# Four partial loads of the next half image, a new order on VectorE, and high parts written by ScalarE in a normalised DCT and ODE-solver kernel

## The chip, the cores and the metric

The kernel runs on one core of one Trainium2 chip. The metric is the device time of one execution in microseconds (us); the median of three runs before is 3626.96 us.

## The reference, cut to what matters

Sixteen images of 32 channels and 112x112 pixels. First a normalised 2-D cosine transform is added to the input, then six Euler steps of a small network with two 3x3 convolutions and three group normalisations (one channel per group, so instance normalisation).

```python
def _L0_conv_ref(x):
    y = jnp.einsum('kh,bchw->bckw', Dh, x)
    return jnp.einsum('lw,bckw->bckl', Dw, y)

def odefunc(t, y):
    h = jax.nn.relu(_group_norm(y, gn1_w, gn1_b))
    h = _concat_conv(t, h, conv1_w, conv1_b)
    h = jax.nn.relu(_group_norm(h, gn2_w, gn2_b))
    h = _concat_conv(t, h, conv2_w, conv2_b)
    return _group_norm(h, gn3_w, gn3_b)

def step(y, t):                       # six times, dt = 1/6
    return (y + dt * odefunc(t, y), None)

x = x + _L0_conv_ref(_gn(x))
x = x + _L1_conv_ref(_gn(x), ...)     # returns y after six steps
```

## The kernel before

**Tiling.** Two images are in work at a time, one in each of two slots; eight groups of two images make the sixteen. An image of a slot lies on 128 partitions as 32 channels times four pixel parities. A convolution is TensorE matmuls over f16 operands. Each activation is held as a high part (f16 of the f32 value) and a low part (f16 of what is left); products high x high, high x low and low x high are summed in PSUM. A convolution call (`convolve`) goes through eight pieces in the order of `PHASES`: X0 X1 Y0 X2 Y1 X3 Y2 Y3, where the number is one of four parts of the image. An X piece has 12 rounds of four matmuls, a Y piece 6. A dict `between` puts other matmuls at a (piece, round). X of part k waits until the low parts up to k+2 (`lo_done`) are there.

**Staging.** `step(g, s, kind)` exists once for each engine; s is the solver step, 0 to 5. Its four convolution calls are: slot 1 conv 1, slot 0 conv 2, slot 1 conv 2, and slot 0 conv 1 of the next solver step. The two slots alternate, so that the normalisation of one is worked out while TensorE convolves the other. For one convolution call the chain is: ScalarE evacuates PSUM to z (`evacuate`); VectorE takes statistics (`pair_stats`), or for conv 2 ScalarE sums squares (`squares`) and VectorE products with y (`products`); TensorE sums them over partitions (`statistics`); VectorE works out scale and bias, with one or two rsqrt on GpSimd (`post`, `post_state`); ScalarE applies scale, bias and relu (`activate`), VectorE subtracts to get the low part (`split`). With `hi=True`, `activate` also writes the f16 high part before it writes the f32 value in place; with `hi=False`, VectorE's `split` makes the high part with a cast.

**Kinds of step.** In the first seven groups steps 0 to 3 are MID: they also carry the transform of one half of a later image (16 channels). This work is: load of xs, `half_stats` (one batch-norm statistics instruction a channel), `half_pre`, `half_post`, `normalise_first` on VectorE for the first four channels and `normalise` on GpSimd for the other twelve, `dct_rows` and `dct_columns` on TensorE in the fourth call, `batch_copy` on ScalarE, and `half_add` (called `added(b)` in the step), which reads xs and writes x1s. Step 4 is FOUR, step 5 FIVE (both prepare the next group's start states). The last group has LAST_MID steps and a LAST.

**Queues.** All DMAs are issued by SyncE, in program order. In each MID step these are `last_piece` (loads of an earlier result half, a wait for VectorE's `last_add`, the out store), `store_half` (L384), which waits until all four `half_add` of the half are done, and `load_half` (L370), which waits for the same and loads all of xs. VectorE waits for it before `half_stats(range(0, 4))`, behind `pre_of(Z1, 0, 9)` and ahead of `post_of(Z1, 0)`. The order on each engine is written out by hand in `step`; every engine is in order.

**Where the lines lie.** Cast of a high part on VectorE L1085, low part L1089, Euler update L1093, products L1101, statistics of xs L1138, `half_add` L1187; on ScalarE evacuation L667, squares L687, high parts L696, relu in f32 L697; `post_state` begins at L1039. TensorE: convolution matmuls L1456, statistics of Z2 L1550, of Z1 L1544.

Of the kernel before, what the change touches and what calls it, by code (L numbers as in the profile page):

```python
# [28 lines left out]
NP = 4  # L29
# [43 lines left out]
HI_ACT, HI_DVE = 10, 6  # L73
# [68 lines left out]
def build(nc, x, wt, w0, par, dct_c, mats_c, coef_c, ind_c, x1d, yd, out):  # L142
# [5 lines left out]
    with ExitStack() as ctx:  # L148
# [107 lines left out]
        xsb_in = sem("xsb_in")  # L256
        s_m0 = sem("s_m0")
# [99 lines left out]
        def _(sp):  # L357
# [9 lines left out]
            def load_half(index, n):  # L367

                sp.wait_ge(x1_done, NBATCH * n + 1)
                sp.dma_start(xs[:], x_half[bass.ds(index, 1)].rearrange("a h c w -> (a h) c w")).then_inc(xs_in, 16)  # L370
# [59 lines left out]
            load_half(HALVES % NHALF, HALVES)  # L430
# [12 lines left out]
            with sp.Fori(0, LG) as g:  # L443
                with sp.Fori(0, HALVES) as s:
                    with sp.If(g > 0):
                        last_piece(g, g * HALVES + s)
                    store_half((g + 1) * HALVES + s)
                    load_half(((g + 1) * HALVES + s + 1) % NHALF, (g + 1) * HALVES + s + 1)
# [45 lines left out]
            sp.wait_ge(xs_in, 16 * (first_place(HALVES * GROUPS) + 1))  # L494
# [154 lines left out]
        def _(act):  # L649
# [96 lines left out]
            def step(g, s, kind):  # L746
# [43 lines left out]
                activate(1, Z1, 0, False)  # L790
                squares(0, 0, c, sq + 0)
                activate(1, Z1, 1, False)
                evacuate(0, 1, s, 1, 1, c)
                activate(1, Z1, 2, False)
                squares(0, 1, c, sq + 1)
                evacuate(0, 1, s, 1, 2, c)
                activate(1, Z1, 3, False)
# [65 lines left out]
        def _(dve):  # L863
# [169 lines left out]
            def post_state(slot, ev, n, covs, meanwhile):  # L1033
# [16 lines left out]
                                               op0=ALU.mult, op1=ALU.subtract, reverse1=True).then_inc(cov_done, 1)  # L1050

# [83 lines left out]
            def half_stats(channels, buffers=FIRST):  # L1135
                src, _, _, bn0, _ = buffers
                for c in channels:
                    ins = nc.vector.bn_stats(bn0[:, c, :], src[:, c, :])  # L1138
                if channels[-1] == CQ - 1:
                    ins.then_inc(s_m0, 1)  # L1140

# [103 lines left out]
            def step(g, s, kind, adds=False):  # L1245
# [19 lines left out]
                def split_for(phase, k):  # L1265
# [3 lines left out]
                    if phase == 1:  # L1269
                        by_act = HI_ACT * u + k  # L1270
                    elif phase == 2:
                        by_dve = 2 * NP + HI_DVE * u + k
                    elif phase == 3 and k < 2:
                        by_dve = 2 * NP + HI_DVE * u + NP + k
                    elif phase == 3:
                        by_act = HI_ACT * u + NP + k - 2
                    else:
                        by_act = HI_ACT * u + NP + 2 + k
                    split(slot, conv, k, conv_at(g, s, phase), by_act, by_dve)

                def update(slot, meanwhile):

                    if keeps:
                        post_state(slot, stats_before(g, s, kind) + STATS[kind].index((Z2, slot)),
                                   posts_before(g, s, kind) + POSTS[kind].index((Z2, slot)),
                                   2 * (5 * g + s) + slot, meanwhile)
# [9 lines left out]
                if kind == MID:  # L1296
                    dve.wait_ge(xs_in, 16 * first_place(hn) + 16)
                    half_stats(range(0, 4))
# [3 lines left out]
                if kind == MID:  # L1302
                    half_stats(range(4, 7))
                split_for(1, 1)
                stats_of(0, 1)
                if kind == MID:
                    half_stats(range(7, 10))
# [38 lines left out]
                if kind == MID:  # L1346
                    normalise_first(hn)
# [3 lines left out]
                euler(0, 2)  # L1351
                if kind == LAST:
                    euler(0, 3)
# [4 lines left out]
                split_for(3, 0)  # L1358
                split_for(3, 1)
                products_of(2, 0)  # L1360
# [57 lines left out]
        def _(pe):  # L1418
# [179 lines left out]
            def step(g, s, kind):  # L1598
# [38 lines left out]
                between = {(1, 10): lambda: statistics_of(Z2, 0)}  # L1637
# [59 lines left out]
```

## Time and profile before

| | before |
|---|---|
| median of 3 runs | 3626.96 us (3626.53 to 3645.11) |
| profiled execution | 3623.7 us |
| its span | 3621.9 us |
| TensorE matmul / weight load busy | 83% / 70% |
| VectorE, ScalarE, GpSimd busy | 75%, 69%, 28% |
| mean granted clock of TensorE | 0.936 |
| DMA | 217.55 MB, mean 60 GB/s |

A matmul's end is modelled, so a busy share of 83% is an upper figure; the start times of matmuls show where TensorE stood. In a timeline, the bracket behind an instruction gives the idle time of its engine before it and the instruction that ended it. A row of the statistics by windows gives the length of a stretch, then the busy time of each engine with its count of instructions.

### The profile page before, as it was taken

To read this page: it belongs to the slowest core of one execution; us is meant where nothing else is said; L and a number is where in the kernel's file an instruction comes from. 1 tells how busy PE (TensorE), PEld (TensorE's weight loads), DVE (VectorE), ACT (ScalarE), POOL (GpSimd) and SP (SyncE) were. 2 spreads that over 40 slices of the span, in tenths; PEclk is the share of its full clock that TensorE was granted. 3 is DMA by queue.
4 is the path that set the end of the run, shared out by engine and by line. 5 is a ranking of instruction groups with operands and counts; after the bars stand their busy time and mean duration, and the time that the engine had idled before them with its cause. 6 is when DMAs were issued, how large, how long until landed. Compare 5 with 4: busy or idle time off the path is not lost.

```text
span 3621.9 us, 147894 instructions
## 1 busy us (share of the span) xinstructions
PE 3012.7 (83%) x61716; PEld 2531.6 (70%) x61716; DVE 2723.5 (75%) x6289; ACT 2497.7 (69%) x3867; POOL 1012.9 (28%) x1293
## 2 busy tenths in 40 slices
PE   3589888888888888888988888888888888889984
PEld 3477777767777677776777767677777676778873
DVE  6577777777777777776877678777886777768883
ACT  0376678666786667866787567866678666787774
POOL 4034411443124331333313333133421344111111
PEclk7799999999999999999999999999999999999997
DMA  4300033111331131322303213141132211330113
GB/s 85 81 21 21 20 56 92 47 47 56 56 93 47 56 79 24 92 63 75 65 3 101 82 47 65 23 116 47 47 65 57 82 47 47 65 91 30 56 47 108
DMA packets 368816, 217.55 MB, mean 60 GB/s; under 512 B 353152, under 2 KB 353520, under 8 KB 366064
## 3 DMA queue, kind: packets, MB, share of 16 engines
q1 hardware_dynamic: 368112, 207.63, 22.9%
q8 instruction: 507, 8.31, 0.9%
q14 instruction: 197, 1.61, 0.1%
HBM read 104.85 MB, written 77.07 MB: 50 GB/s over the span
## 4 chain that ended last, share of the span: by engine, by line
issue 40%; DVE 17%; ACT 14%; PE 12%; POOL 11%; DMA 3%; SPq 2%; POOLq 1%; DVEq 0%; ACTq 0%
PE cps L1456 8%; ACT z L697 5%; ACT z L667 4%; DVE y L1093 3%; POOL m L547 3%; DVE ha L1089 2%; SPq L439 2%; DVE hb L1089 2%; POOL small L504 2%; POOL ha L535 2%; DMA y<-xa 1%; PE dps L1564 1%; ACT unread_z L687 1%; DVE unread_yz L1101 1%; ACT y L760 1%
## 5 line engine op out<-in xcount | busy, mean ns | idle before, releaser
L1456 PE MATMUL cps<-ha,w 64*64 64x392 f16 (+1 forms) x27648 | 1382.2, 343 | 134.8 <-DVE ha L1089 104.3
L1456 PE MATMUL cps<-hb,w 64*64 64x392 f16 x27648 | 1308.4, 339 | 173.9 <-DVE hb L1089 148.5
L1456 PEld LDWEIGHTS cps<-hb,w 64*64 64x64 f16 x27648 | 1093.9, 109 | 296.9 <-issue 188.0
L1456 PEld LDWEIGHTS cps<-ha,w 64*64 64x64 f16 x27648 | 1063.9, 109 | 323.7 <-issue 160.6
L667 ACT ACTIVATE z<-cps,bias_now 128x784 f32<-128x784 f32 (+2 forms) x1056 | 762.4, 738 | 614.6 <-PE cps L1456 606.2
L504 POOL TENSOR_TENSOR small<-small,half 128x1 f32<-128x1 f32 x304 | 168.5, 554 | 1777.1 <-DVE small L1020 1393.7
L1119 DVE BATCH_NORM_STATS2 bnt<-z 128x6 f32<-128x392 f32 (+1 forms) x768 | 390.0, 551 | 132.3 <-ACT z L667 131.4
L1089 DVE TENSOR_TENSOR hb<-z,hb 128x784 f16<-128x784 f32 x384 | 375.2, 977 | 100.1 <-ACT z L697 92.0
L1089 DVE TENSOR_TENSOR ha<-z,ha 128x784 f16<-128x784 f32 x384 | 378.8, 987 | 87.3 <-ACT z L697 83.1
L560 POOL TENSOR_SCALAR xn<-xs,m 112x112 f32<-112x112 f32 x336 | 399.0, 1198 | 5.8 <-POOL xn L560 5.8
L697 ACT ACTIVATE z<-z,small 128x784 f32<-128x784 f32 x384 | 395.9, 1031 | 3.9 <-DVE small L1029 3.2
L1093 DVE SCALAR_TENSOR_TENSOR y<-z,small,y 128x784 f32<-128x784 f32 x384 | 397.6, 1048 | 0.1
L1479 PE MATMUL cps<-rim_i,rim_now 64*64 64x7 f16 (+1 forms) x3072 | 376.5, 170 | 0.0
L697 ACT ACTIVATE z<-y,small 128x784 f32<-128x784 f32 x320 | 329.1, 1032 | 53.4 <-DVE small L1076 52.6
L1101 DVE SCALAR_TENSOR_TENSOR unread_yz<-z,y 128x784 bf16<-128x784 f32 x320 | 305.6, 978 | 38.2 <-DMA y<-xa 31.5
L687 ACT ACTIVATE unread_z<-z 128x784 bf16<-128x784 f32 x384 | 324.8, 848 | 4.8
L696 ACT ACTIVATE hb<-z,small 128x784 f16<-128x784 f32 x192 | 198.9, 1036 | 143.8 <-DVE small L1029 143.8
L1479 PEld LDWEIGHTS cps<-rim_i,rim_now 64*64 64x64 f16 x3072 | 278.7, 108 | 25.6 <-issue 2.6
L696 ACT ACTIVATE ha<-y,small 128x784 f16<-128x784 f32 x240 | 249.3, 1039 | 22.6 <-DVE small L1076 14.1
L1138 DVE BATCH_NORM_STATS2 bn<-xs 112x6 f32<-112x112 f32 x480 | 97.8, 263 | 192.1 <-DMA xs<-in_x_dram 192.1
L535 POOL COPY ha<-ha 64x112 f16<-64x112 f16 x96 | 115.5, 1203 | 240.6 <-DVE ha L1089 229.7
L1564 PE MATMUL dps<-dct,xn 112*112 112x112 f32 x896 | 121.5, 281 | 54.6 <-DVE x1s L1187 53.6
(162 smaller groups left out, 2666.4 us busy)
## 6 DMA issues: line engine op xcount, KB each, us to landing
xa<-x_dram SPq DMA_DIRECT2D x128, 196.0 KB, 5.0
y<-xa SPq DMA_DIRECT2D x16, 1568.0 KB, 7.6
y_dram<-y SPq DMA_DIRECT2D x128, 196.0 KB, 4.7
xs<-in_x_dram SPq DMA_DIRECT2D x31, 784.0 KB, 8.5
x_dram<-x1s SPq DMA_DIRECT2D x30, 784.0 KB, 5.3
fin<-y_dram SPq DMA_DIRECT2D x30, 784.0 KB, 8.0
fin<-x_dram SPq DMA_DIRECT2D x28, 784.0 KB, 8.5
out_dram<-fin SPq DMA_DIRECT2D x28, 784.0 KB, 3.3
```

Source lines behind the costliest of these rows:

```text
L504: nc.gpsimd.tensor_tensor(col(small, slot, at, RSTD), col(small, slot, at, VE), half[:, 0:1], ALU.pow).then_inc(pow_done, 1)
L560: last = nc.gpsimd.tensor_scalar(xn[:, c, :], xs[:, c, :], m0[:, 4, c:c + 1], m0[:, 6, CQ + c:CQ + c + 1], ALU.mult, ALU.add)
L667: return nc.scalar.activation(dst, src, ACT.Identity, bias=bias_now[parts, conv:conv + 1], **more)
L687: nc.scalar.activation(unread_z[:, k % 2], part(z[slot], k), ACT.Square, accum_out=zsum[:, slot, k, 1:2]).then_inc(sq_done, 1)
L696: nc.scalar.activation(dst, part_rows(src, k), ACT.Relu, **coefs).then_inc(hi_act, 1)
L697: nc.scalar.activation(part(z[slot], k), part(src, k), ACT.Relu, **coefs).then_inc(r_done, 1)
L1089: nc.vector.tensor_tensor(lo, src, hi, ALU.subtract).then_inc(lo_done, 1)
L1093: nc.vector.scalar_tensor_tensor(out=part(y[slot], k), in0=part(z[slot], k), scalar=col(small, slot, Z2, SC), in1=part(y[slot], k), op0=AL ...
L1101: nc.vector.scalar_tensor_tensor(out=unread_yz[:, k % 2], in0=part(z[slot], k), scalar=2.0, in1=part(y[slot], k), op0=ALU.mult, op1=ALU.mu ...
L1119: nc.vector.bn_stats(bn[slot][:, 2 * k + n, :], z[slot][:, at:at + m])
L1456: return pe.matmul(dst, w[hin * 64:(hin + 1) * 64, kx, a, wl, :], src[:, :, 0:NA], start=(what == "X" and n == 0), stop=(what == "Y" and n ...
L1479: pe.matmul(cps[hout * 64:(hout + 1) * 64, edge:edge + (rows - 1) * NA + 1:NA], rim, rim_i[0:64, COLUMN:COLUMN + rows], start=False, stop= ...
```

## The change

SyncE: `load_half` is replaced by `load_part(index, n, b)`, four channels each, with a semaphore of its own for each b. Part b waits only for `half_add(b)` of the half before. Parts 0 to 2 are issued ahead of `store_half`, part 3 behind it. VectorE: statistics of xs go in four batches of four channels, each behind a wait for its part; `normalise_first` moves from ahead of `update(0)` to behind the second `split` of the fourth call; `euler(0, 2)` moves behind the first; `added(0)` moves from the second wait for rsqrt in `post_state` of slot 1 to the first, and `euler(1, 0)` takes its place. ScalarE: the four `activate(1, Z1, k, False)` become `hi=True`, and the casts of these parts leave VectorE's `split`. TensorE: the statistics of Z2 of slot 0 move from round 10 to round 3 of the second piece of the third call.

```diff
-HI_ACT, HI_DVE = 10, 6
+HI_ACT, HI_DVE = 14, 2
-            def load_half(index, n):
-                sp.wait_ge(x1_done, NBATCH * n + 1)
-                sp.dma_start(xs[:], x_half[bass.ds(index, 1)].rearrange("a h c w -> (a h) c w")).then_inc(xs_in, 16)
+            def load_part(index, n, b):
+                sp.wait_ge(x1_done, NBATCH * (n - 1) + b + 2)
+                sp.dma_start(xs[:, 4 * b:4 * b + 4, :],
+                             x_half[bass.ds(index, 1), :, 4 * b:4 * b + 4].rearrange("a h c w -> (a h) c w")
+                             ).then_inc(xs_part[b], 16)
...
+                    after = (g + 1) * HALVES + s + 1
+                    for b in range(NBATCH - 1):
+                        load_part(after % NHALF, after, b)
                     store_half((g + 1) * HALVES + s)
-                    load_half(((g + 1) * HALVES + s + 1) % NHALF, (g + 1) * HALVES + s + 1)
+                    load_part(after % NHALF, after, NBATCH - 1)
...
-                activate(1, Z1, 0, False)
+                activate(1, Z1, 0)
...
+                if early:
+                    early()
                 dve.wait_ge(pow_done, n + 1)
...
+            def half_batch(b, n):
+                dve.wait_ge(xs_part[b], 16 * (n - HALVES + 1))
+                half_stats(range(4 * b, 4 * b + 4))
...
-                    dve.wait_ge(xs_in, 16 * first_place(hn) + 16)
-                    half_stats(range(0, 4))
+                    half_batch(0, hn)
                 post_of(Z1, 0)
                 stats_of(0, 0)
                 split_for(1, 0)
                 if kind == MID:
-                    half_stats(range(4, 7))
+                    half_batch(1, hn)
                 split_for(1, 1)
                 stats_of(0, 1)
                 if kind == MID:
-                    half_stats(range(7, 10))
+                    half_batch(2, hn)
...
-                if kind == MID:
-                    half_stats(range(10, 13))
-                post_of(Z1, 1, meanwhile=(lambda: half_stats(range(13, CQ))) if kind == MID else None)
+                post_of(Z1, 1, meanwhile=(lambda: half_batch(3, hn)) if kind == MID else None)
...
                 split_for(2, 3)
-                if kind == MID:
-                    normalise_first(hn)
                 update(0, lambda: euler(0, 0))
                 euler(0, 1)
-                euler(0, 2)
...
                 split_for(3, 0)
+                euler(0, 2)
                 split_for(3, 1)
+                if kind == MID:
+                    normalise_first(hn)
...
-                update(1, (lambda: added(0)) if kind == MID else lambda: euler(1, 0))
-                if kind == MID:
-                    euler(1, 0)
+                update(1, lambda: euler(1, 0), (lambda: added(0)) if kind == MID else None)
...
-                between = {(1, 10): lambda: statistics_of(Z2, 0)}
+                between = {(1, 3): lambda: statistics_of(Z2, 0)}
```

## Rows read from the trace of the kernel before

**Rows 1.** Busy time by windows of one step: length, PE PEld DVE ACT POOL, clock, DMA.
```profile
1035.40:1110.90 75.50, 66.36 (x1306) 54.93 (x1306) 59.70 (x142) 55.33 (x87) 28.70 (x32) 0.95 0.38 102
1187.00:1264.20 77.20, 65.05 (x1307) 53.53 (x1306) 58.52 (x141) 49.94 (x81) 28.29 (x32) 0.93 0.18 54
1264.20:1340.40 76.20, 65.84 (x1307) 53.94 (x1306) 58.43 (x141) 49.97 (x81) 28.07 (x32) 0.93 0.18 55
1340.40:1401.30 60.90, 53.93 (x1248) 47.80 (x1249) 49.47 (x109) 43.05 (x70) 8.32 (x18) 1.00 0.45 82
1401.30:1472.10 70.80, 56.99 (x1246) 48.27 (x1247) 49.69 (x107) 64.62 (x90) 8.61 (x20) 0.98 0.11 22
3408.30:3468.10 59.80, 53.50 (x1242) 47.55 (x1242) 50.46 (x106) 47.59 (x77) 10.09 (x18) 1.00 0.12 43
```

**Rows 2.** The same by convolution call: A of a MID; A and C of a FOUR.
```profile
1187.00:1207.40 20.40, 13.51 (x311) 11.85 (x311) 7.75 (x25) 7.38 (x11) 1.46 (x5) 0.89 0.56 159
...
1340.40:1353.60 13.20, 13.20 (x312) 11.85 (x313) 7.16 (x18) 7.84 (x12) 1.46 (x5) 1.00 0.70 164
...
1367.00:1385.20 18.20, 13.56 (x323) 11.95 (x320) 16.92 (x38) 11.50 (x22) 2.42 (x4) 1.00 0.18 31
```

**Rows 3.** Waits over the whole span: total us, times, longest.
```profile
DVE bn L1138 <- DMA xs<-in_x_dram: 192.1, 22, 9.9
```

**Rows 4.** Timelines of VectorE and of TensorE: start, us, instruction, idle before.
```profile
1199.54 0.81 DVE L1138 BATCH_NORM_STATS2 bn<-xs 112x6 f32<-112x112 f32 x4 [9.67 <-DMA xs<-in_x_dram]
...
1207.42 4.09 PE L1456 MATMUL cps<-hb,w 64*64 64x392 f16 x45 [6.91 <-DVE hb L1089]
```

**Rows 5.** Windows of TensorE behind that wait: length, busy, granted clock, DMA.
```profile
1208.00:1210.00 2.00, 2.00 (x28) 0.50 0.03 8
```

**Rows 6.** DMA issues: engine, count, KB each, median us to landing.
```profile
xa<-x_dram SPq DMA_DIRECT2D x128, 196.0 KB, 5.0
...
xs<-in_x_dram SPq DMA_DIRECT2D x31, 784.0 KB, 8.5
```

**Rows 7.** Timeline of SyncE's queue late in the 77.2 us step.
```profile
1260.08 0.36 SPq L409 DMA_DIRECT2D out_dram<-fin  x1
```

**Rows 8.** Groups of instructions by line and shape: busy us, mean ns.
```profile
L1085 DVE CAST hb<-z 128x784 f16<-128x784 f32 x192 | 111.1, 579 | 21.9 <-ACT z L697 21.4
```

**Rows 9.** Timelines of a LAST_MID step: ScalarE, and TensorE's start of B.
```profile
3419.18 1.04 ACT L696 ACTIVATE hb<-z,small 128x784 f16<-128x784 f32 x1
3420.12 1.03 ACT L697 ACTIVATE z<-z,small 128x784 f32<-128x784 f32 x1
...
3432.58 1.04 ACT L697 ACTIVATE z<-z,small 128x784 f32<-128x784 f32 x1
...
3441.51 0.85 ACT L687 ACTIVATE unread_z<-z 128x784 bf16<-128x784 f32 x1
...
3425.06 1.71 PE L1456 MATMUL cps<-hb,w 64*64 64x392 f16 x35
```

**Rows 10.** Timelines: statistics of Z2, LAST_MID on both engines, then a FOUR.
```profile
3442.60 0.36 PE L1550 MATMUL sps<-zsum,mats 128*128 128x12 f32 x2
...
3443.20 0.17 DVE L1039 TENSOR_REDUCE small<-sps 128x3 f32<-128x12 f32 x1
...
1374.58 0.39 PE L1550 MATMUL sps<-zsum,mats 128*128 128x12 f32 x2 [2.75 <-DVE unread_yz L1101]
```

**Rows 11.** Timelines of the 77.2 us step: slot 0's update to D, third add.
```profile
1229.00 0.17 DVE L1039 TENSOR_REDUCE small<-sps 128x3 f32<-128x12 f32 x1
...
1238.56 2.11 PE L1456 MATMUL cps<-ha,w 64*64 64x448 f16 x42 [1.98 <-DVE ha L1089]
...
1259.97 0.62 DVE L1187 TENSOR_TENSOR x1s<-dps,xs 112x448 f32<-112x448 f32 x1
```

**Rows 12.** Timeline of VectorE in the first MID of a group.
```profile
1064.38 0.98 DVE L1101 SCALAR_TENSOR_TENSOR unread_yz<-z,y 128x784 bf16<-128x784 f32 x1 [4.42 <-DMA y<-xa]
```

**Rows 13.** Window of ScalarE in a FIVE: length, busy, clock, DMA.
```profile
999.80:1041.10 41.30, 40.59 (x60) 0.96 0.25 53
```

More of the change, by code:

```diff
@@ L256, in build @@
         xsb_in = sem("xsb_in")
+        xs_part = [sem(f"xs_part{b}") for b in range(NBATCH)]
         s_m0 = sem("s_m0")
@@ L429, in _ @@
                 load_start(image, image)
-            load_half(HALVES % NHALF, HALVES)
+            for b in range(NBATCH):
+                load_part(HALVES % NHALF, HALVES, b)
             for slot in range(SLOTS):
@@ L493, in _ @@
                 sp.wait_ge(xa_in[slot], 128 * GROUPS)
-            sp.wait_ge(xs_in, 16 * (first_place(HALVES * GROUPS) + 1))
+            sp.wait_ge(xs_in, 16 * SLOTS)
+            for b in range(NBATCH):
+                sp.wait_ge(xs_part[b], 16 * (HALVES * (GROUPS - 1) + 1))
             sp.wait_ge(x1_out, 16 * first_place(HALVES * GROUPS) + 16)
@@ L789, in step @@
                 act.wait_ge(post_done, posted(Z1, 1))
-                activate(1, Z1, 0, False)
+                activate(1, Z1, 0)
                 squares(0, 0, c, sq + 0)
-                activate(1, Z1, 1, False)
+                activate(1, Z1, 1)
                 evacuate(0, 1, s, 1, 1, c)
-                activate(1, Z1, 2, False)
+                activate(1, Z1, 2)
                 squares(0, 1, c, sq + 1)
                 evacuate(0, 1, s, 1, 2, c)
-                activate(1, Z1, 3, False)
+                activate(1, Z1, 3)
                 evacuate(0, 1, s, 1, 3, c)
@@ L1031, in post, with post_state @@
                                                op0=ALU.mult, op1=ALU.subtract, reverse1=True).then_inc(post_done, 1)
-            def post_state(slot, ev, n, covs, meanwhile):
+            def post_state(slot, ev, n, covs, meanwhile, early):
                 done, mine = NPOST * n, NCOV * covs
@@ L1271, in split_for, with update @@
                     elif phase == 2:
+                        by_act = HI_ACT * u + NP + k
+                    elif phase == 3 and k < 2:
                         by_dve = 2 * NP + HI_DVE * u + k
-                    elif phase == 3 and k < 2:
-                        by_dve = 2 * NP + HI_DVE * u + NP + k
                     elif phase == 3:
-                        by_act = HI_ACT * u + NP + k - 2
+                        by_act = HI_ACT * u + 2 * NP + k - 2
                     else:
-                        by_act = HI_ACT * u + NP + 2 + k
+                        by_act = HI_ACT * u + 2 * NP + 2 + k
                     split(slot, conv, k, conv_at(g, s, phase), by_act, by_dve)
-                def update(slot, meanwhile):
+                def update(slot, meanwhile, early=None):
                     if keeps:
@@ L1285, in update @@
                                    posts_before(g, s, kind) + POSTS[kind].index((Z2, slot)),
-                                   2 * (5 * g + s) + slot, meanwhile)
+                                   2 * (5 * g + s) + slot, meanwhile, early)
                         return
@@ L1358, in step @@
                 split_for(3, 0)
+                euler(0, 2)
                 split_for(3, 1)
+                if kind == MID:
+                    normalise_first(hn)
                 products_of(2, 0)
```

## The prediction

> **What bounds the kernel now.** I read the waits first, then the steps one by one, then the timelines of the engines in one step. I call the four convolutions of a solver step A (slot 1, first conv), B (slot 0, second conv), C (slot 1, second conv) and D (slot 0, first conv of the next step). There are 48 steps: 28 carry the transform of a later half image (MID; 4 in each of 7 groups), 7 are FOUR, 7 FIVE, 5 LAST_MID, 1 LAST. Representative lengths: 75.5 us for the first MID of a group, 77.2 and 76.2 for two later ones, 60.9 FOUR, 70.8 FIVE, 59.8 LAST_MID [rows 1]. No engine is full: in the 77.2 us step VectorE is busy 58.5, ScalarE 49.9, TensorE 65.1 by modelled ends. So the time is a chain of hand-overs, and the phases say where TensorE waits [rows 2]: A alone can take 13.2 (the FOUR step), and takes 20.4 in the MID step. There VectorE stands 9.67 us at the batch statistics of xs until the load has landed, and TensorE then waits 6.91 for B's first low parts [rows 4]. The wait adds up to 192.1 us in 22 places [rows 3]: 21 are the second to fourth MID of each group, one is at the start. After the gap the clock is granted at 0.50, the 1.2 GHz level [rows 5], so B begins slowly too.
>
> **Partial loads.** The load is issued today after the last add and after the store, and takes a median 8.5 us for 784 KB; a 196 KB transfer takes 5.0 [rows 6]. After the change parts 0 and 1 leave SP as soon as `last_piece` lets SP go. Its out store is issued at 1260.08, 4.1 us before A of the next step begins at 1264.2 [rows 1, 7]. I let VectorE ask for part 0 at A+2.9, so there are 6 to 7 us for a 5.0 us landing beside an out store. It does not need the statistics of A's normalisation until A+5.3, so 2 us more would be hidden. Part 3 is issued behind the store at about A+3 and wanted only at about A+19.5. Issuing three more DMAs costs SP about 1 us, and SP waits most of the step anyway. The split loads therefore cost nothing and end the wait: A goes to 13.1 and B's slow start goes. If the parts land 3 us later than I think, 1 us a step comes back.
>
> **ScalarE writes C's high parts.** VectorE loses four casts of 0.579 us a step, 2.3 us [rows 8]; ScalarE gains four of its activations. One begins 0.94 after the one before [rows 9], so 3.74 us. These stand in phase B in front of evacuations and squares. From the first relu to the end of the last square ScalarE works almost without a gap: 3432.58 to 3442.35, 9.8 us [rows 9]. It becomes 13.5. TensorE's statistics of C need that last square, and the new state of slot 0, hence D, hangs on them. In the LAST_MID step they run at 3442.60 and VectorE takes them up at 3443.20 [rows 10].
>
> Rows alone say a cast costs 0.58 where it is and 0.94 where it goes, on an engine whose work is in the chain here. The Trainium skill, "Perfetto Trace Analysis", section Optimizing Scalar/DVE Operations, says that work which both engines can do is faster in VectorE's performance mode and that moving it to ScalarE may make sense when VectorE is saturated. VectorE at 58.5 of 77.2 us is not; by that rule this edit should cost and the sum below stands, while a saturated VectorE gives the first rival.
>
> **Statistics of Z2 at round 3 instead of 10.** Seven rounds of four matmuls, about 1.3 us. It gives something only if the squares are done by then. They will not be: the wait moves forward and 1.3 us of matmuls, once in front of it, come behind. What remains of C after the statistics is about 10 us, and from VectorE's first step of that chain (1229.00) to D's first matmul (1238.56) it is 9.6 today [rows 11], so D is then started by TensorE as much as by the chain. **Reordering on VectorE**: `normalise_first` (1.1 us) leaves the path to D's first parts and goes where TensorE needs it only 2 us after D starts: up to 1.1 us gained in MID, none where squares are last. Moving `euler(0,2)` changes the order, not the time of the second part. `added(0)` in the first wait for rsqrt (0.44 idle) and `euler(1,0)` in the second give about 0.5.
>
> **MID, second to fourth**, times from A's start. A ends 13.1 (B's low parts ready at 12). B has the normalisation of slot 1 to wait for: in the LAST_MID step ScalarE's first relu comes 7.5 after B's start (3425.06 to 3432.58) [rows 9]; with the last four channels inside VectorE's rsqrt wait I put it at B+7.6, 20.7. ScalarE from there: 13.5 plus a little, last square at 34.4. VectorE: low parts of C at 23.5 and 26.3, so C starts at 26.4, and the last product is done at 33.8. TensorE holds at C's statistics from about 29 to 34.8, with one wait of 1.5 for an evacuation in front. It would end C at 44.8; a gap that long gives one slow stretch, as in rows 5, for which I add 2: 47. D starts there; the slot 1 chain is taken up at about 52.7. VectorE takes up the slot 0 statistics at 1229.00 today and begins the third of its adds at 1259.97, 31 us later [rows 11], and the step ends 3.7 us after that add. With the new order both routes, this one from 35.2 and TensorE's from 47, end at 71 to 71.5. I take 71.4 against 76.2: 4.8 x 21 = 101 us gained. Bounds: 3 us (TensorE cold for longer) and 6 (never cold), 63 to 126.
>
> **MID, first of a group.** No wait for xs; VectorE stands 4.42 us for the new y instead [rows 12], and that stays. Fewer casts bring C's start 1 us forward, ScalarE's end of squares stays just within; 1.6 x 7 = 11 us.
>
> **FOUR.** TensorE waits 2.75 for products today [rows 10]; with start statistics between them VectorE ends them at the same time. 1.3 us of matmuls and a slow stretch come behind the wait, partly taken up by the wait for D: 1.5 x 7 = 10 us lost (0 to 3 each).
> **FIVE.** ScalarE is busy 40.6 of 41.3 us from late in B into the next A [rows 13]. Four activations more go straight through: 3.7 to 4, x 7 = 28 lost.
> **LAST_MID and LAST.** Last square 3.74 later, C's rest behind it: C ends 4.1 later, D 4 to 5: 28 lost over six steps.
>
> Sum: -101 -11 +10 +28 +28 = -46 us. The profiled execution took 3623.7 (span 3621.9), 3 us below the median 3626.96: profile 3578, **median 3581**.
>
> **Rivals.** (1) ScalarE's additions are covered, VectorE is what binds: then MID gains 5.5 to 6 and the other kinds nothing: about -125, 3502. For it: VectorE has 2.3 us less to do in each step, and it is the releaser in most waits. Against: the gapless row of ScalarE [rows 9, 13]. (2) The moved statistics stop TensorE so long that the clock stays at 0.50 over most of C, and D starts 3 us later than I say in all 47 steps that have a C before a D: MID gains only 1.8, the others lose 3 us more: +40, **3667, slower**. [...] (3) The parts queue behind the out store and VectorE still waits 4 us past A+2.9: 2.5 to 3 us of A's gain lost in 21 steps, about +58 on my sum: 3639, no change. Against: 784 KB land in 8.5 us even beside a store.
>
> **Chances.** Forecast case (3545 to 3609) 0.53; rival 1 0.19; rival 2 0.10; rival 3 0.12; the rest, mixed, 0.06, is spread. The measurement tells about 0.5%, 18 us, from no change. Faster by more than that (below 3609): 0.74; within: 0.15; slower: 0.11. The range takes in part of rivals 1 and 3: 3515 to 3637.
>
> **What the profile will show.** The row of VectorE waiting for xs below 20 us in all; A at 13.1 to 13.5 in every MID; TensorE's statistics of C with a wait of 3 to 6 us on ScalarE's squares in every kind of step, and VectorE's wait for B's parts gone; LAST_MID at 64; FIVE at 74.5; MID at 71.4; FOUR near 62. VectorE's casts of hb (192) are gone, ScalarE's `hb<-z` activations double to 384. I am wrong if ScalarE's extra work is not seen in the wait in C (then LAST_MID stays at 60), or if a wait for parts remains.

## The result: slower, and the profile after

The changed kernel takes a median of 3707.05 us (four runs, 3697.25 to 3713.72), the kernel before 3636.03 beside it on the same chip: ratio 1.0191 [1.0146, 1.0237]. The forecast was 3581, so even the sign was wrong. The profiled execution took 3706.5 us, span 3704.7, mean clock 0.925. Its busy times:

```profile
PE 3079.3 (83%) x61716; PEld 2558.8 (69%) x61716; DVE 2620.0 (71%) x6097; ACT 2670.6 (72%) x4059; POOL 789.7 (21%) x1293
```

These are windows of one step each, to set against [rows 1] (length, then busy time and instructions of PE, PEld, DVE, ACT and POOL, then clock, DMA share, GB/s): a later MID (second to fourth of its group), a FOUR, a FIVE and a LAST_MID.

```profile
1197.60:1273.20 75.60, 66.91 (x1311) 54.63 (x1310) 56.37 (x136) 53.32 (x85) 19.54 (x32) 0.93 0.18 56
1348.60:1413.60 65.00, 57.75 (x1247) 49.33 (x1246) 47.89 (x106) 47.48 (x75) 8.23 (x18) 0.92 0.41 68
1413.60:1490.40 76.80, 58.72 (x1247) 48.60 (x1247) 46.77 (x101) 67.91 (x93) 8.51 (x20) 0.96 0.11 21
3467.60:3536.00 68.40, 59.44 (x1238) 50.76 (x1242) 48.83 (x103) 51.54 (x81) 9.14 (x18) 0.90 0.10 38
```

The MID window is barely shorter than before, the other three are 4 to 9 us longer. Means over all steps of a kind, from TensorE's first matmul of A to the next A, give the budget:

| kind | steps | before, us | after, us | difference x steps | forecast |
|---|---|---|---|---|---|
| MID, second to fourth | 21 | 76.34 | 74.79 | -33 | -101 |
| MID, first of a group | 7 | 74.69 | 76.44 | +12 | -11 |
| FOUR | 7 | 61.14 | 64.86 | +26 | +10 |
| FIVE | 7 | 70.51 | 76.85 | +44 | +28 |
| LAST_MID | 5 | 61.53 | 67.71 | +31 | +28 with LAST |
| LAST | 1 | 93.94 | 101.38 | +7 | |
| ahead of the first A | | 172.7 | 167.0 | -6 | |

The differences add up to +83, which is that of the spans, 3704.7 - 3621.9. The sum in the prediction was -46, so the miss is 129 us, and 68 of them lie in the 21 later MID steps. By convolutions, the MID step at 1197.60:

```profile
1197.60:1210.70 13.10, 13.10 (x309) 11.77 (x312) 8.45 (x25) 7.54 (x12) 1.47 (x5) 1.00 0.65 203
1210.70:1224.60 13.90, 13.52 (x324) 11.94 (x318) 11.20 (x37) 12.03 (x18) 1.47 (x5) 1.00 0.02 5
1224.60:1245.30 20.70, 16.29 (x321) 13.10 (x313) 13.70 (x32) 14.19 (x26) 10.76 (x14) 0.84 0.01 2
1245.30:1273.20 27.90, 24.00 (x378) 17.82 (x378) 23.03 (x45) 19.56 (x32) 5.84 (x8) 0.94 0.17 52
```

A, which took 20.4 in [rows 2], takes 13.1; C has become 20.7. The parts of the load land in time, and VectorE takes part 0 without a wait, against 9.67 us in [rows 4] (its timeline):

```profile
1200.19 0.80 DVE L1149 BATCH_NORM_STATS2 bn<-xs 112x6 f32<-112x112 f32 x4
```

and the issues have the smaller DMAs (KB each, median us to landing):

```profile
xs<-in_x_dram SPq DMA_DIRECT2D x116, 196.0 KB, 4.5
```

What took the place of [rows 3] among the waits (total us, times, longest) is TensorE at the statistics of Z2, most of it for ScalarE's squares. The weight load (PEld) and the matmul (PE) of one statistic can stand at the same wait, so the first two rows are not to be added. Before, the same four stood at 22.3, 11.2, 49.8 and 7.0 us; after, they are:

```profile
PEld sps L1562 <- ACT unread_z L696: 179.5, 56, 4.3
PE sps L1562 <- ACT unread_z L696: 140.8, 47, 3.8
PE sps L1562 <- DVE unread_yz L1112: 92.1, 47, 3.9
...
ACT ha L705 <- DVE y L1104: 43.9, 66, 0.9
```

### The profile page after: what moved, and what is told of

Read it like the earlier page. It is cut to its first block, busy times and chain, and to the rows that moved or that the text cites. A ratio compares the mean times of both kernels' runs of the same rounds, so it can differ in the third digit from the quotient of the medians.

```text
span 3704.7 us, 148287 instructions
## 1 busy us (share of the span) xinstructions
PE 3079.3 (83%) x61716; PEld 2558.8 (69%) x61716; DVE 2620.0 (71%) x6097; ACT 2670.6 (72%) x4059; POOL 789.7 (21%) x1293
## 4 chain that ended last, share of the span: by engine, by line
issue 26%; ACT 25%; PE 21%; DVE 19%; DMA 3%; POOL 3%; SPq 2%; DVEq 0%; POOLq 0%; ACTq 0%
PE cps L1468 16%; ACT z L706 9%; ACT z L676 7%; ACT hb L705 3%; ACT unread_z L696 3%; DVE y L1104 3%; DVE unread_yz L1112 3%; SPq L443 2%; DVE ha L1100 2%; PE dps L1584 2%; PE dps L1576 2%; DVE bnt L1130 2%; DMA y<-xa 1%; ACT ha L705 1%; ACT y L769 1%
## 5 line engine op out<-in xcount | busy, mean ns | idle before, releaser
L1468 PE MATMUL cps<-hb,w 64*64 64x392 f16 x27648 | 1361.8, 347 | 67.8 <-ACT z L676 32.9
L1468 PEld LDWEIGHTS cps<-hb,w 64*64 64x64 f16 x27648 | 1107.7, 112 | 220.2 <-issue 84.8
L705 ACT ACTIVATE hb<-z,small 128x784 f16<-128x784 f32 x384 | 398.0, 1037 | 1.5
L1491 PE MATMUL cps<-rim_i,rim_now 64*64 64x7 f16 (+1 forms) x3072 | 385.7, 172 | 0.0
L1562 PE MATMUL sps<-zsum,mats 128*128 128x12 f32 x192 | 45.6, 312 | 232.9 <-ACT unread_z L696 140.8
L1562 PEld LDWEIGHTS sps<-zsum,mats 128*128 128x128 f32 x192 | 36.6, 238 | 270.0 <-ACT unread_z L696 179.5
L569 POOL TENSOR_SCALAR xn<-xs,m 112x112 f32<-112x112 f32 x336 | 202.3, 615 | 5.8 <-POOL xn L569 5.8
```

What stands on the lines that cost most here:

```text
L569: last = nc.gpsimd.tensor_scalar(xn[:, c, :], xs[:, c, :], m0[:, 4, c:c + 1], m0[:, 6, CQ + c:CQ + c + 1], ALU.mult, ALU.add)
L705: nc.scalar.activation(dst, part_rows(src, k), ACT.Relu, **coefs).then_inc(hi_act, 1)
L1468: return pe.matmul(dst, w[hin * 64:(hin + 1) * 64, kx, a, wl, :], src[:, :, 0:NA], start=(what == "X" and n == 0), stop=(what == "Y" and n ...
L1491: pe.matmul(cps[hout * 64:(hout + 1) * 64, edge:edge + (rows - 1) * NA + 1:NA], rim, rim_i[0:64, COLUMN:COLUMN + rows], start=False, stop= ...
```

## Where the later MID step loses its gain

I followed the step through its engines. TensorE's timeline, in C:

```profile
1231.99 0.60 PE L1562 MATMUL sps<-zsum,mats 128*128 128x12 f32 x2 [3.64 <-ACT unread_z L696]
```

The same stretch in windows of 2 us, TensorE alone (length, busy, granted clock, DMA share, GB/s):

```profile
1232.00:1234.00 2.00, 2.00 (x22) 0.50 0.00 0
1234.00:1236.00 2.00, 2.00 (x34) 0.50 0.03 8
1236.00:1238.00 2.00, 2.00 (x36) 0.54 0.00 0
```

ScalarE's last square ends at 1232.0, TensorE has stood 3.64 us for it, and the next 6 us are granted at 0.50 to 0.54, the 1.2 GHz level. So C's first pair of PSUM tiles, the results of its first part of the image, is finished late. Now ScalarE, whose queue holds the evacuation of that pair, its squares, and only then the relu of slot 0's new state:

```profile
1237.86 0.91 ACT L676 ACTIVATE z<-cps,bias_now 128x784 f32<-128x784 f32 x1 [5.63 <-PE cps L1468]
...
1239.83 1.96 ACT L706 ACTIVATE z<-y,small 128x784 f32<-128x784 f32 x2
```

And VectorE, which made the relu's bias and waits for the relu:

```profile
1232.63 0.17 DVE L1048 TENSOR_REDUCE small<-sps 128x3 f32<-128x12 f32 x1 [0.38 <-PE sps L1562]
...
1236.41 0.23 DVE L1087 SCALAR_TENSOR_TENSOR small<-small,gb 128x1 f32<-128x1 f32 x1
...
1240.89 0.57 DVE L1096 CAST ha<-z 128x784 f16<-128x784 f32 x1 [3.18 <-ACT z L706]
...
1252.61 0.17 DVE L1048 TENSOR_REDUCE small<-sps 128x3 f32<-128x12 f32 x1
...
1267.35 0.62 DVE L1203 TENSOR_TENSOR x1s<-dps,xs 112x448 f32<-112x448 f32 x1
```

The bias is there at 1236.64 and the relu starts at 1239.83: it needs nothing of C's first pair, but stands behind the pair's evacuation and its squares. From slot 0's statistics to the third add VectorE takes 34.7 us here, against 31.0 in [rows 11]. The one wait is 3.18; `normalise_first`, which now stands inside this stretch, is another 1.1, and shorter waits elsewhere take some of it back. TensorE waits twice more in D, for products and for an add that both come late:

```profile
1251.62 0.39 PE L1562 MATMUL sps<-zsum,mats 128*128 128x12 f32 x2 [1.62 <-DVE unread_yz L1112]
...
1268.10 1.44 PE L1576 MATMUL dps<-dct,xn 112*112 112x112 f32 x8 [1.93 <-DVE x1s L1203]
```

Windows of TensorE behind that second wait:

```profile
1268.00:1270.00 2.00, 1.90 (x18) 0.64 0.89 351
1270.00:1272.00 2.00, 2.00 (x37) 0.51 1.03 264
```

My theory for the tests: ScalarE's four added activations and the early statistics together make a hold in C, and ScalarE's own order carries it into VectorE's chain. The rivals: the hold is TensorE's alone (rival 2), VectorE's reordering is what costs, or the partial loads bring less than forecast.

## Each part alone

**The loads alone.** Run e1: the kernel before with the four partial loads.

```diff
-                    load_half(((g + 1) * HALVES + s + 1) % NHALF, (g + 1) * HALVES + s + 1)
+                    for b in range(NBATCH - 1): load_part(after % NHALF, after, b)   # ahead of store_half
+                    load_part(after % NHALF, after, NBATCH - 1)                      # behind it
```

> Only the partial loads and the four batches of statistics; casts on VectorE, its order and the statistics of Z2 at round 10 as before. Theory (the loads are worth what the waits say, the loss comes from the other edits): A falls to 13.1 us in the second to fourth MID, as in the changed kernel, C and D are not held by squares; a MID step comes to 69 to 71 us against 76.7, some 6.5 x 21 = 140 us less: about 3490. Rival (the time of A was only slack of VectorE's chain and is given back in D, whatever the other edits do): MID stays at 75, about 3600.

3461.71 us, ratio 0.9518 [0.9502, 0.9535]: 174 us gained, more than the 140 expected. A later MID takes 68.84 us in the mean, 7.5 less than before. Windows of one of them: whole, then its A, C and D:

```profile
1135.40:1203.70 68.30, 62.31 (x1311) 52.32 (x1311) 58.30 (x140) 49.24 (x80) 28.19 (x32) 1.00 0.18 58
1135.40:1148.50 13.10, 13.10 (x309) 11.77 (x312) 8.39 (x25) 6.99 (x11) 1.47 (x5) 1.00 0.64 203
...
1162.40:1177.90 15.50, 13.26 (x321) 11.78 (x312) 14.61 (x35) 11.56 (x22) 11.01 (x10) 1.00 0.01 2
1177.90:1203.70 25.80, 22.42 (x378) 16.78 (x379) 22.30 (x42) 18.80 (x31) 13.02 (x13) 1.00 0.14 46
```

ScalarE's timeline in that C:

```profile
1168.44 0.92 ACT L676 ACTIVATE z<-cps,bias_now 128x784 f32<-128x784 f32 x1 [1.90 <-PE cps L1469]
...
1172.40 2.12 ACT L706 ACTIVATE z<-y,small 128x784 f32<-128x784 f32 x2 [1.90 <-DVE small L1087]
```

The clock is full throughout. C's first pair is evacuated at 1168.44, 4 us ahead of the relu, and the relu waits for its own bias: here ScalarE's order is the right one. The Trainium skill, "DMA: Bandwidth & Descriptors", section Rules for kernel authors, advises merging small transfers into one large one and draws its line at 64 KB. At 196 KB the parts are above it, and nothing here speaks against the rule: four loads bring the first batch of channels in a median 4.5 us instead of 8.5 [rows 6], and nobody waits for the rest.

The shorter transfer is the smaller part of it. In the traces of before and of e1, over the 21 later MID steps, the median issue of what VectorE wants first moves from A+3.1 to A-3.4, and its landing from A+11.7 to A+0.3; VectorE asks for it at A+2.8. So 6.5 of the 11.4 us come from the earlier issue, which needs only a quarter of the adds and does not stand behind the store. No run splits the load without issuing it earlier, or lets VectorE ask later for a whole one.

**ScalarE's writes alone.** Run e2.

```diff
-                activate(1, Z1, 0, False)
+                activate(1, Z1, 0)          # the same for k = 1, 2, 3; VectorE's four casts go
```

> Only the four high parts of C on ScalarE instead of VectorE's casts; loads, order and statistics as before. Theory (four activations stand ahead of the squares on ScalarE): 3.7 us in each of the 47 steps whose new state hangs on the squares, +130 to +170, about 3780, most plainly in FIVE and LAST_MID, which have no transform. Rival (the extra work is covered on ScalarE, and the loss of the changed kernel is the early place of the statistics): 3600 to 3640.

3736.05 us, 1.0291 [1.0252, 1.0329]: by the medians 100 us lost, less than the 144 expected but well clear of a gain. C grows from 15.3 to 18.3 in the later MID, FIVE by 3.4, LAST_MID by 3.9. This is the rows' price (0.94 on ScalarE against 0.58 on VectorE) plus the hold. The rule cited in the forecast from the Trainium skill, "Perfetto Trace Analysis", section Optimizing Scalar/DVE Operations, that moving work to ScalarE may pay once VectorE is saturated, agrees with this run from its other side: at 58.5 of 77.2 us busy [rows 1] VectorE is not saturated, and the move costs 2.9%.

**The statistics at round 3 alone.** Run e3.

```diff
-                between = {(1, 10): lambda: statistics_of(Z2, 0)}
+                between = {(1, 3): lambda: statistics_of(Z2, 0)}
```

> Only the statistics of Z2 of slot 0 at round 3 instead of 10 of C's second piece. Theory (without ScalarE's extra work the squares come just at round 10, so the hold is only 1.3 us and D's start has some slack): -10 to +40, about 3640. Rival (the early place is what costs, as the matmuls behind it and ScalarE's evacuation come late): +100 or more, 3730.

3642.09 us, 1.002 [1.0005, 1.0035]: as expected, about nothing in all. By kinds it is not nothing: FOUR, where TensorE waits for products at that place [rows 10], goes from 61.14 to 63.09 in the mean, FIVE from 70.51 to 71.47, and the later MID from 76.34 to 75.98.

**VectorE's order alone.** Run e4: `euler(0, 2)` and `normalise_first` later, `added(0)` and `euler(1, 0)` earlier.

```diff
-                if kind == MID:
-                    normalise_first(hn)
                 products_of(1, 0)
...
-                euler(0, 2)
                 split_for(3, 0)
+                euler(0, 2)
                 split_for(3, 1)
+                if kind == MID:
+                    normalise_first(hn)
...
-                update(1, (lambda: added(0)) if kind == MID else lambda: euler(1, 0))
+                update(1, lambda: euler(1, 0), (lambda: added(0)) if kind == MID else None)
```

> Only VectorE's new order (normalise_first, euler(0,2), added(0), euler(1,0)). Theory: up to 1.1 us less in each of 28 MID steps on the way to D, 0 to -30 us, about 3610. Rival (normalise_first behind the second split delays the products of C and with them the statistics in D): +20 to +40, 3660.

3668.92 us, 1.0081 [1.005, 1.0111]: 33 us lost where I expected a gain of 26. Two runs take it apart: e13 moves `euler(0, 2)` alone, e14 `normalise_first` alone.

```diff
-                euler(0, 2)
                 split_for(3, 0)
+                euler(0, 2)
```

> Only euler(0,2) behind the first split of D, all else as before. Theory (ScalarE's relu of part 2 waits for it, with the square and evacuations of C queued behind, so the squares that D's statistics need come later; felt in LAST_MID too, which has no transform): +0.5 us in each step, about +25, 3660. Rival (it only changes the order of two things of equal length, as predicted, and the loss of the new order is normalise_first): 3630 to 3640.

3667.23 us, 1.009 [1.0058, 1.0123]: by the medians 30 us, nearly the whole. Among the waits of e13, the row of ScalarE's third parts says how; it stood at 7.0 us in 21 places before and is

```profile
ACT ha L696 <- DVE y L1095: 44.9, 65, 0.9
```

ScalarE makes D's third part from this y. VectorE gets to it one split later, ScalarE stands 0.7 us at it in 65 places, and squares and evacuations stand behind it in its queue. LAST_MID, which has no transform, is 0.8 us longer too, as the theory had it.

```diff
-                if kind == MID:
-                    normalise_first(hn)
                 products_of(1, 0)
...
                 split_for(3, 1)
+                if kind == MID:
+                    normalise_first(hn)
```

> Only normalise_first behind D's second split. Theory (D starts up to 1 us earlier, but the products of C come 1 us later against it: neither a gain nor a loss over 0.3%): 3625 to 3645. Rival (it is the part of the new order that costs): 3655 to 3665.

3655.6 us, 1.0062 [1.0041, 1.0082]: 18 us lost. In the later MID, D starts sooner but is longer: C goes from 15.3 to 14.5, D from 26.0 to 28.1, the step from 76.3 to 77.5. FOUR, FIVE and LAST_MID stay. `normalise_first` now stands ahead of the products of C, for which TensorE waits in D: among the waits of e14 that row, 49.8 us in 32 places before, is

```profile
PE sps L1552 <- DVE unread_yz L1103: 87.0, 47, 2.8
```

The two sum to 48, more than e4's 33; each has an uncertainty of 8 to 12 us, so what `added(0)` and `euler(1, 0)` give back, if anything, is not resolved.

## The parts in pairs

**Loads with ScalarE's writes.** Run e5: e1 with the edit of e2.

```diff
+                    load_part(...)              # as in e1
+                activate(1, Z1, k)              # as in e2
```

> Partial loads and high parts of C on ScalarE; order and statistics (round 10) as before. The loads alone measured 3462, ScalarE's parts alone +100. Theory (the squares end 3.7 us later and the loads leave no other wait to hide it in): C 18 to 18.5 us in MID against 15.5 with the loads alone, about 3570. Rival (the two edits make each other worse, the interaction seen in the changed kernel is between them): MID near 75, 3620 or more.

3565.21 us, 0.9805 [0.9775, 0.9835]: 103 above e1, as e2 was 100 above before.

**Loads with the early statistics.** Run e6.

```diff
+                    load_part(...)              # as in e1
+                between = {(1, 3): lambda: statistics_of(Z2, 0)}
```

> Partial loads and the statistics of Z2 at round 3; casts on VectorE, order as before. Theory (the early place costs little while the squares are in time; about +0.2% alone): 3465 to 3480. Rival (the early place and the loads hurt each other, since C now comes sooner after B's squares): C up by 2 us in MID, 3520.

3462.32 us, 0.952 [0.9488, 0.9553]: equal to e1. As in e3 the kinds differ: FOUR is 1.8 us longer than in e1 (62.64 against 60.89), the later MID 0.7 shorter (68.10 against 68.84). The place of the statistics is worth nothing in the sum here, and not because nobody waits.

**After with the statistics back at round 10.** Run e7.

```diff
-                between = {(1, 3): lambda: statistics_of(Z2, 0)}
+                between = {(1, 10): lambda: statistics_of(Z2, 0)}
```

> The changed kernel with the statistics of Z2 back at round 10. Theory (round 3 behind late squares puts 1.3 us of matmuls and a slow stretch behind the wait, 2 us in each C): C falls from 20.6 to 18.5 in MID, FIVE and LAST_MID, about 90 us less than the changed kernel: 3610 to 3620. Rival (the place does not matter, the wait is for the squares in any case): 3690 to 3710.

3604.09 us, 0.9902 [0.9876, 0.9929]: 103 us back from one number. Here ScalarE's four added activations are still there, and the squares late. Among its waits, the row of TensorE's matmuls for them is

```profile
PE sps L1562 <- ACT unread_z L696: 97.0, 46, 2.9
```

against 140.8 above: 44 us of the 103 are in the waits themselves, the rest is what follows on them.

**After with the casts back on VectorE.** Run e8.

```diff
-                activate(1, Z1, 0)
+                activate(1, Z1, 0, False)   # k = 0 to 3; four casts back on VectorE
```

> The changed kernel with the casts of C's high parts back on VectorE. Theory (ScalarE's four activations before the squares are the largest loss, 3 us alone and 5 with the early statistics): 3500 to 3515, 200 us less than the changed kernel. Rival (the losses only add as measured alone): 3707 less 105, 3600.

3512.98 us, 0.9665 [0.9638, 0.9691]: 194 us back. It is the largest single piece.

**After with VectorE's old order.** Run e9: the edit of e4 undone.

```diff
+                euler(0, 2)                 # ahead of split_for(3, 0) again
+                    normalise_first(hn)     # ahead of products_of(1, 0) again
```

> The changed kernel with VectorE's old order: partial loads, ScalarE's high parts, statistics at round 3. Together with the loads and ScalarE's parts (3565) it prices the early statistics when the squares are late and the order is old. Theory (the early place costs by itself 2 us a C once squares are late, with any order): 3640 to 3660. Rival (it costs only with the new order, where D's VectorE work also comes late): 3560 to 3580.

3660.3 us, 1.0072 [1.0048, 1.0097]: the order costs 47 us in the company of the rest.

So, from medians: loads -174; ScalarE's writes +100 alone, +103 on top of the loads; the early statistics 0 without those writes and +95 (e9 less e5) to +103 with them; the order +33 alone, 39 to 51 in company. Going from before by way of e1, e5 and e9 to the changed kernel, the steps are -174, +103, +95 and +47, which is +71 in all. The same four steps by kinds, means from the profiled executions in us:

| kind | before | e1: loads | e5: and ScalarE's writes | e9: and statistics at round 3 | after: and VectorE's order |
|---|---|---|---|---|---|
| MID, second to fourth | 76.34 | 68.84 | 71.31 | 73.63 | 74.79 |
| MID, first of a group | 74.69 | 75.29 | 74.92 | 74.75 | 76.44 |
| FOUR | 61.14 | 60.89 | 61.38 | 63.49 | 64.86 |
| FIVE | 70.51 | 70.45 | 74.16 | 76.43 | 76.85 |
| LAST_MID | 61.53 | 61.90 | 64.79 | 66.21 | 67.71 |

The first MID of a group, which the loads hardly touch, scatters by 0.6 us between them; smaller differences are not read.

## ScalarE's order: the test of the theory

**`normalise_first` back.** Run e10: after with it ahead of `update(0)`, since I first took D's 27.9 us for its work.

```diff
+                if kind == MID:
+                    normalise_first(hn)
                 update(0, lambda: euler(0, 0))
```

> The changed kernel with normalise_first back ahead of update(0), where it now stands in VectorE's wait for the late squares; euler(0,2) and added(0) keep their new places. Theory (of the new order it is normalise_first that delays the products of C, and so the statistics in D): D in MID falls by 1 to 2 us, 28 steps, 3650 to 3670. Rival (euler(0,2) between the splits is what delays): 3700.

3696.92 us, 1.0172 [1.0144, 1.0201]: only 10 us. That reason fell for the later MID, which goes from 74.79 to 74.48. The first MID of a group goes from 76.44 to 74.79, where it was before the change: there `normalise_first` is the reason.

**The relu ahead of the evacuation.** Run e15: after with ScalarE's two relus of slot 0's new state drawn forward; nothing is added, removed or made faster.

```diff
+                state_part(0, 0, False)
                 evacuate(1, 1, s, 2, 0, c)
+                state_part(0, 1, False)
                 squares(1, 0, c, sq + 4)
-                state_part(0, 0, False)
-                state_part(0, 1, False)
```

> The changed kernel with ScalarE's relu of the new state (first part) ahead of its evacuation and square of C's first pair, so that it does not wait for matmuls behind the held statistics. Theory (that queue carries the hold on to VectorE, D's statistics and the end of D: 3.2 us wait of the first cast of D): MID 75.3 down to about 73.5, the other kinds 1 less, 3640 to 3660. Rival (D is started by TensorE, which has 10 us of C behind the statistics at half clock in part; the order on ScalarE changes nothing): 3695 to 3710.

3598.28 us, 0.9907 [0.9879, 0.9934]: 109 us from the order of four calls, twice what I expected. Windows of a later MID: whole, its C, its D:

```profile
1164.90:1236.50 71.60, 64.72 (x1307) 53.63 (x1306) 56.74 (x137) 53.55 (x85) 22.55 (x32) 0.95 0.19 59
...
1191.90:1211.80 19.90, 15.64 (x320) 12.86 (x314) 16.04 (x37) 15.14 (x29) 13.15 (x14) 0.83 0.01 2
1211.80:1236.50 24.70, 22.46 (x384) 17.02 (x376) 21.00 (x40) 18.62 (x29) 6.47 (x9) 1.00 0.14 47
```

ScalarE's timeline there:

```profile
1203.93 1.04 ACT L706 ACTIVATE z<-y,small 128x784 f32<-128x784 f32 x1 [4.43 <-DVE small L1090]
```

C still has its hold and its slow clock (19.9 us at 0.83); D is 24.7, against the 24.4 between the forecast's 47 and 71.4. The relu now waits for its own bias. Means: later MID 71.39, first MID 75.09, FOUR 62.84, FIVE 76.06, LAST_MID 66.34. Of the 109 us, 71 are in the 21 later MID steps (3.40 each), 14 in FOUR.

**The same order where C's first pair is early.** Run e16: e1 with the edit of e15.

```diff
+                    load_part(...)              # as in e1
+                state_part(0, 0, False)         # as in e15
```

> The partial loads alone, with ScalarE's relu of the new state's first part ahead of its evacuation and square of C's first pair. Here the statistics stand at round 10 and the pair is ready 4 us before the relu may start. Theory (the queue cost something only where matmuls behind the held statistics came late, so nothing is to be had here, and the evacuation comes later than it could): 3462 to 3500. Rival (the order is better in any case): 3430 or less.

3526.64 us, 0.97 [0.9677, 0.9723], 65 us worse than e1: the sign turns. Now ScalarE stands at the relu while the pair lies finished, and evacuates it behind:

```profile
1190.38 1.04 ACT L706 ACTIVATE z<-y,small 128x784 f32<-128x784 f32 x1 [5.84 <-DVE small L1090]
...
1191.32 0.89 ACT L676 ACTIVATE z<-cps,bias_now 128x784 f32<-128x784 f32 x1
```

C becomes 17.1 us against 15.5 in the mean. The order is right for whichever input comes first, and the change had swapped them: bias first in the changed kernel, C's pair first in e1.

## Attempts to go below e1

Run e11: e6 with only `added(0)` and `euler(1, 0)` early.

```diff
-                update(1, (lambda: added(0)) if kind == MID else lambda: euler(1, 0))
+                update(1, lambda: euler(1, 0), (lambda: added(0)) if kind == MID else None)
```

> Partial loads, statistics at round 3, added(0) in the first and euler(1,0) in the second wait for rsqrt; casts on VectorE, euler(0,2) and normalise_first in their old places. Theory (the filled waits are worth 0.3 to 0.5 us in MID): 3450 to 3462. Rival (no gain): 3462 to 3475.

3466.55 us, 0.9536 [0.9515, 0.9558]: equal to e1 and e6. These two moves are worth nothing either way.

Run e12: e11, and GpSimd normalises the first four channels in VectorE's place.

```diff
+                for c in range(4):
+                    last = nc.gpsimd.tensor_scalar(xn[:, c, :], xs[:, c, :], ...)
+                last.then_inc(xn_first, 1)
-                if kind == MID: normalise_first(hn)
```

> As the run before, but GpSimd normalises the first four channels too, right behind the half's bias, and normalise_first is gone from VectorE. Theory (VectorE's 1.1 us ahead of the update is on the way to D, and GpSimd is free from the half's bias to the rsqrt): 1 us a MID step less, 3425 to 3440. Rival (GpSimd's four operations at 1.2 us each end after the rsqrt is wanted): 3470 to 3500.

3459.74 us, 0.9516 [0.9495, 0.9537]: a miss. VectorE's 1.1 us a step had no buyer there.

Run e17: e12 with ScalarE's order of e15.

```diff
+                state_part(0, 0, False)         # as in e15, in the kernel of e12
```

> Partial loads, statistics at round 3, casts on VectorE, all normalisation on GpSimd, and ScalarE's new order of relu and evacuation. Theory: the pair is ready only after the statistics, about when scale and bias are; 3440 to 3470. Rival (the hold reaches D through ScalarE here too): 3400 to 3430.

3496.03 us, 0.9615 [0.9592, 0.9638]: 36 worse than e12, the sign of e16, and a miss: in e12 the pair's evacuation starts 2.5 us ahead of the relu (1156.70 and 1159.21 in its trace), so there too the pair is first. The best kernels are e1, e6 and e12, which can't be told apart: 3460 to 3462 us, 4.8% below before. The partial loads alone are the version to keep.

## Why the prediction was wrong

- **Partial loads: right, and too low.** A at 13.1, the wait gone (5.0 us left, at the start of the kernel), B's slow start gone. Three more issues cost SyncE some 2 us, not 1, and it had the room. The forecast had them only together with what comes behind; alone they are worth 7.5 us a later MID.
- **ScalarE's writes: right in place, in size and in its first consequence.** A at 13.1, B 13.9 (forecast C's start at A+26.4, measured A+27.0), the last square at A+34.4 as forecast, slot 0's statistics taken up at A+35.0 (forecast 35.2), D's start at A+47.7 (47).
- **The step that failed is the clause that from there "this one from 35.2 and TensorE's from 47, end at 71 to 71.5".** I gave TensorE a slow stretch of 2 us and let VectorE's chain run at its old 31 us, or 32 with `normalise_first` in it. The hold and the slow stretch delay C's first pair; its evacuation and squares stand ahead of the relu in ScalarE's order; VectorE's chain takes 34.7. The statistics of D are taken up at A+55.0 instead of 52.7: 2.3 us. From them to the third add it takes 14.7 us, against 14.9 before. From the add to the end it is 5.85 instead of 3.7, in TensorE's slow stretch there. Together they turn 71.4 into 75.6, the window above. With the relu ahead of the evacuation the same step takes 71.4 in the mean (e15), and those 3.4 us in 21 steps, 71 us, cover the 68 that the later MID missed its forecast by. That run shows the cause of the first term; that the second goes with it is seen (D at clock 1.00), but not why, since a wait of 1.92 us is still there.
- **First MID of a group: wrong sign, and by another edit than I feared.** I had put in doubt only ScalarE's squares, "just within", and they hold: with the writes (e5) the step takes 74.92, with the statistics at round 3 as well (e9) 74.75, against 74.69 before. VectorE's new order brings it to 76.44 and D from 26.0 to 28.3; with `normalise_first` alone put back (e10) it is 74.79 again. The forecast -11 was +12.
- **FIVE, FOUR, LAST_MID: right mechanism, sizes too small.** FIVE 6.3 against 4, FOUR 3.7 against 1.5, LAST_MID 6.2 against 4 to 5. e5 has FIVE +3.7 and LAST_MID +3.3 with the writes and the old place of the statistics, where the activations "go straight through" as forecast. The early statistics add 2.3 in FIVE and 1.4 in LAST_MID, the order 0.4 and 1.5. In FOUR the early statistics cost 2.0 even alone (e3), close to the forecast 1.5, and the order 1.4, which was not in the sum. On top of late squares the early statistics, priced at 1.3 us of matmuls and a slow stretch in FOUR, cost 95 to 103 us over the kernel, 2.3 us a step or more in the later MID.
- **Reordering on VectorE: wrong.** Forecast up to 1.5 us a MID gained, measured 33 us lost. "Moving `euler(0,2)` changes the order, not the time" looked at VectorE alone; ScalarE needs that y. And `normalise_first` went out of a place where it cost nothing I could find (e12) into one ahead of the products that TensorE waits for.
- **The rivals.** Rival 2 had the slower side and the moved statistics, with 0.10. Its price was added up wrongly: with 1.8 gained in the 21 later MID steps and 3 us more lost in the other 26 of its 47, its own terms give +95 and 3722, and not +40 and 3667. Its mechanism was not the one either: D started at A+47.7, 0.7 later than forecast, not 3. What was missing is that a delay of TensorE comes back through ScalarE. So that the measured 3707 lies near the corrected 3722 is luck. Rival 3 fell: no part was late.

Under most of these points lies one: squares that come late together with statistics that come early are in the later MID, in FIVE and in LAST_MID, and I priced their consequence once, as 2 us of TensorE in one kind. VectorE's order, which I had as a gain, is the other. The range had been made as if each kind could go wrong by itself.

## What to carry to other kernels

- When an engine is held, follow not only who waits for it but what stands behind the delayed instruction in the queue of every engine that it feeds. An instruction whose own inputs are ready can be the one that sets the end; here it was a relu, ready 3.2 us before it ran.
- A fixed order in a queue encodes which input arrives first. In e1 C's first pair is evacuated 3.9 us ahead of the bias (1168.44 and 1172.37), in the changed kernel 1.2 us behind it (1237.86 and 1236.64). A change that shifts two arrivals by 5 us against each other can turn the right order into the wrong one: the same swap gave 109 us in one kernel and took 65 in another.
- Parts of a change are to be priced alone. The one that removed a 192 us wait was worth 174; the ones that came with it to use the room cost 245 together. A part that is worth nothing in all can still be a gain in one kind of step and a loss in another (e3, e6).

## What was not expected of the hardware

**GpSimd's pace hangs on what VectorE does beside it.** Its 336 normalisations of 112x112 have the same code in both kernels. The groups of before and of after:

```profile
L560 POOL TENSOR_SCALAR xn<-xs,m 112x112 f32<-112x112 f32 x336 | 399.0, 1198 | 5.8 <-POOL xn L560 5.8
```

```profile
L569 POOL TENSOR_SCALAR xn<-xs,m 112x112 f32<-112x112 f32 x336 | 202.3, 615 | 5.8 <-POOL xn L569 5.8
```

1198 ns against 615. In the timelines of the two MID steps four of them take 7.92 us while VectorE works without a gap (from 1236.09, before) and 1.70 us while it stands for the relu (from 1238.65, after). The Trainium skill, "Perfetto Trace Analysis", section Optimizing Scalar/DVE Operations, says that the two engines share a read port of their memory; the rows agree in kind, though spans on GpSimd are rough. Of the 336 in the changed kernel, 119 ran with VectorE idle for over four fifths of their time and took 432 to 442 ns each; before there are none such, and the longest took 2755. VectorE's busy share alone does not set the pace: in e15, where only two have VectorE idle beside them, the mean is 789. Which of VectorE's instructions slow GpSimd down no run separates.

**The clock after a gap.** A wait of 3.64 us on TensorE is followed by 6 us at 1.2 GHz. In the changed kernel one of 1.93 us is followed by 0.64 and 0.51; in e15, behind 1.92 us at the same place, the clock stays at 1.00. What decides between them I leave open.
